# Attention tiles of a fused layer: one set of four transposes moved behind the first block of a projection, another set moved ahead of a projection

## What is computed

```
q, k, v = x @ Wq, x @ Wk, x @ Wv            # 16 heads of 32
q, k = rotate(silu(q)), rotate(silu(k))
# in chunks of 128 rows, with a running state S per head
scores = (q_i @ k_i.T) * D
o_i    = scores @ v_i + (q_i * decay_q) @ S
S      = lam_C * S + (k_i * decay_k).T @ v_i
o = group_rmsnorm(o * sigmoid(x @ Wg1 @ Wg2)) * weight
x = x + o @ Wo
# feed-forward: 512 -> 4096 (gate and up, 4-bit weights) -> 512
x = x + (gelu(gate) * up) @ Wdown
```

## Time and profile before

| | |
|---|---|
| median of three runs | 1288.63 us |
| profiled execution | 1288.75 us, of which the span from first to last instruction 1286.7 us |
| TensorE busy | 1270.3 us (99%) |
| VectorE busy | 917.0 us (71%) |
| ScalarE busy | 475.2 us (37%) |
| GpSimd busy | 435.2 us (34%) |
| granted TensorE clock | 1.00 over the span |
| attention part | about 9 to 310 us |

### The profile page before, as it was taken

The page is one execution under the profiler, slowest core; times in us unless marked ns, Lnnn a source line. Parts: engine busy times, 40 slices in busy tenths (PEclk is TensorE's granted clock), DMA queues, the critical chain, the costliest instruction groups (busy, mean ns, idle before and its releaser), DMA issues.

```text
span 1286.7 us, 20699 instructions
## 1 busy us (share of the span) xinstructions
PE 1270.3 (99%) x7376; PEld 1043.5 (81%) x7376; DVE 917.0 (71%) x1594; ACT 475.2 (37%) x799; POOL 435.2 (34%) x360
## 2 busy tenths in 40 slices
PE   9999999998999999999999999999999999999998
PEld 6888888887788888888888888888888888888887
DVE  7878788788867667676767676767767666767665
ACT  5433434434433333333333433333333333333421
POOL 2434455564442322223132324133232324232400
PEclk9999999999999999999999999999999999999999
DMA  9000000000001000010000000001001000000003
GB/s 326 12 2 1 19 17 2 2 1 2 25 25 33 17 33 27 22 33 28 29 24 24 24 24 24 33 16 33 24 24 33 24 33 24 24 24 24 24 13 119
DMA packets 21778, 40.23 MB, mean 31 GB/s; under 512 B 2660, under 2 KB 2916, under 8 KB 21604
## 3 DMA queue, kind: packets, MB, share of 16 engines
q1 hardware_dynamic: 21060, 39.47, 9.4%
q10 hardware_dynamic: 672, 0.13, 0.1%
HBM read 35.40 MB, written 4.19 MB: 31 GB/s over the span
## 4 chain that ended last, share of the span: by engine, by line
PE 93%; DVE 2%; POOL 1%; ACT 1%; issue 1%; POOLq 0%; DVEq 0%; ACTq 0%
PE bank L1351 16%; PE bank L1354 15%; PE bank L1353 15%; PE bank L1197 13%; PE bank L1199 13%; PE bank L1198 13%; PE bank L1211 2%; PE bank L1291 1%; PE bank L1310 1%; PE bank L1300 1%; PE bank L1343 1%; PE bank L1331 1%; PE bank L1258 0%; ACT xg L394 0%; PE bank L1257 0%
## 5 line engine op out<-in xcount | busy, mean ns | idle before, releaser
L883 DVE TENSOR_TENSOR acc<-acc,bank 128x512 f32<-128x512 f32 x248 | 169.3, 683 | 129.4 <-PE bank L1199 129.3
L1197 PE MATMUL bank<-wdh,hh 128*128 128x512 f32 x512 | 199.3, 389 | 0.0
L1199 PE MATMUL bank<-wdh,hl 128*128 128x512 f32 x512 | 199.2, 389 | 0.0
L1198 PE MATMUL bank<-wdl,hh 128*128 128x512 f32 x512 | 199.2, 389 | 0.0
L1351 PE MATMUL bank<-xoh,wgh 128*128 128x512 f32 x448 | 175.9, 393 | 0.6 <-DVE cxa L891 0.6
L1351 PE MATMUL bank<-xoh,wuh 128*128 128x512 f32 x448 | 175.1, 391 | 0.7 <-ACT cxa L482 0.7
L1354 PE MATMUL bank<-xoh,wgl 128*128 128x512 f32 x448 | 174.5, 390 | 0.0
L1354 PE MATMUL bank<-xoh,wul 128*128 128x512 f32 x448 | 174.3, 389 | 0.0
L1353 PE MATMUL bank<-xol,wuh 128*128 128x512 f32 x448 | 174.3, 389 | 0.0
L1353 PE MATMUL bank<-xol,wgh 128*128 128x512 f32 x448 | 174.3, 389 | 0.0
L899 DVE TENSOR_TENSOR hl<-hx,hh 128x512 fp32r<-128x512 f32 x128 | 113.5, 887 | 51.4 <-ACT hh L489 51.0
(11 more groups left out here) (163 smaller groups left out, 2285.7 us busy)
## 6 DMA issues: line engine op xcount, KB each, us to landing
stg<-packed_dram SPq DMA_DIRECT2D x48, 256.0 KB, 2.5
stg<-scales_dram SPq DMA_DIRECT2D x48, 256.0 KB
out_dram<-acc SPq DMA_DIRECT2D x16, 256.0 KB, 2.0
acc<-x_dram SPq DMA_DIRECT2D x3, 1024.0 KB, 15.0
w_in<-wq_dram SPq DMA_DIRECT2D x2, 512.0 KB, 5.2
w_in<-wk_dram SPq DMA_DIRECT2D x2, 512.0 KB, 6.9
w_in<-wv_dram SPq DMA_DIRECT2D x2, 512.0 KB, 8.6
w_in<-wo_dram SPq DMA_DIRECT2D x2, 512.0 KB, 11.2
```

The lines of the kernel that those rows point to most:

```text
L883: V.tensor_tensor(row, row, BY[j % 2][:], ALU.add).then_inc(y_add, 1)
L1197: pe.matmul(dst, w_h, x_h, start=start, stop=False)
L1198: pe.matmul(dst, w_h, x_l, start=False, stop=False)
L1199: return pe.matmul(dst, w_l, x_h, start=False, stop=stop)
```

## The change

`o_back(t)` of a tile with c below 3 moves from ahead of the q projection of tile t+2 to behind its first block of three matmuls. (Tile 0 has an order of its own, which stays; where c is 3 it stays behind the second block.) `o_transpose(t-1)` moves from behind the v projection of tile t+1 to ahead of it, in tiles 1 to 13; `passage` already has it there for tile 14. On ScalarE the copy `ot_hi_(t-1)` moves ahead of `v_copy(t+1)`, and on VectorE `gate_low(t+1)` moves behind `rope_of`, both from tile 1 on. No instruction is added or removed.

```
 ScalarE, tile(b, c)
                 if at_start(b, c):
                     xt_hi_(2)
+                else:
+                    ot_hi_(t - 1)
                 v_copy(t + 1, (c + 1) % 2)
                 if not at_start(b, c):
-                    ot_hi_(t - 1)
                     xt_hi_(t + 2)
 VectorE, tile(b, c)
                 decayed_q(t)
-                gate_low(t + 1)
                 if at_start(b, c):
+                    gate_low(t + 1)
                     xt_lo_(2)
                 rope_of(b, c, t + 1, (c + 1) % CHUNKS)
+                if not at_start(b, c):
+                    gate_low(t + 1)
                 if not at_start(b, c):
                     ot_lo_(t - 1)
 TensorE, tile(b, c)
                 else:
+                    o_transpose(t - 1)
                     pe.wait_ge(st_done, kvs(b, c))
                 v_project(t + 1)
-                if not at_start(b, c):
-                    o_transpose(t - 1)
...
-                if c < CHUNKS - 1:
-                    o_back(t)
                 q_ready(t + 2)
                 for k in range(KT):
-                    if c == CHUNKS - 1 and k == 2:
+                    if k == (1 if c < CHUNKS - 1 else 2):
                         o_back(t)
                     q_part(k)
```

## The result

The changed kernel takes 1294.78 us (median of 6 runs, 1292.77 to 1295.47), the kernel before 1288.72 on the same chip (6 runs, 1288.38 to 1292.15). The ratio is 1.0039, with a 95% interval of 1.0026 to 1.0051: slower by 0.39%. The profiled execution took 1295.47 us with a span of 1293.4, against 1288.75 and 1286.7; that is 6.7 us more, and the following reading accounts for these 6.7.

What follows compares the result with a forecast made beforehand. TensorE's queue was taken as the bound (busy 1270.3 us, VectorE 917.0). New waits of 8.4 us less gains of 5.2 gave +3.1 us, 1291.8 us against the median of 1288.63; range 1288.2 to 1293.4.

Steps and rivals of the forecast that it cites:

- `o_back`'s wait: At `o_back` in ten tiles, the 0.42 us wait for ScalarE's copy vanishes; net about 0.39 us saved a tile.
- Gains: On TensorE: 3.9 us from `o_back`, 0.85 from `o_transpose`, 0.47 ahead of tile 8's output projection and scores; 5.2 us.
- The new waits: `o_transpose` ahead of the v projection waits for the multiply writing `sq` in tiles 1, 5, 8, 10, 13, 14; 8.4 us.
- The double hold in tile 10: GpSimd's rotation holds VectorE's last small Newton step, then its second half holds the multiply; TensorE waits 3.88 us.
- The row of tile 12: Trace example of a held VectorE small step: 0.66 us instead of 0.17 beside GpSimd's sum.
- `gate_low` behind `rope_of`: On VectorE, `gate_low` ends 1.6 to 2.8 us after the silu, scores start 2.8 after it; no time added.
- The sum: Whole kernel: waits 8.4 us less gains 5.2, net +3.1 us, giving 1291.8; feed-forward part only starts later.
- One hold or none: Fewer GpSimd holds in tiles 8 and 10: +1.7 us with one each, -0.3 with none; chance 0.37.
- The multiply in time: VectorE's chain comes forward with TensorE, so all six waits vanish; about 1283.8 us, chance 0.11.
- `o_back` still waiting: Dearer q projection restart takes up to 3.9 us from the gains, ending at 1295.7; small chance within the 0.52 for slower.

Runs made afterwards that it cites:

- the stands filled: Changed kernel plus 9 and 15 extra unread matmuls just before `o_transpose` in tiles 8 and 10, keeping TensorE busy; 1291.39 us, ratio 1.0022.
- the repeat: The changed kernel measured once more with no edit; 1292.88 us, ratio 1.0036 against the kernel before.
- the fastest kernel: Changed kernel with `o_transpose` late in tiles 1, 5, 8, 10, 13 and the passage, and GpSimd's rotation waiting for the multiply in tile 10; 1284.46 us.

## Why the prediction was right in direction and wrong in size

- **`o_back`'s wait.** Right. It is gone in all ten tiles; 0.42 us a tile instead of the 0.39 forecast.
- **Gains.** 5.87 us came out against 5.2. `o_back` gave 0.3 more. The x transposes now take 0.41 us up to the output projection in every tile, instead of 0.47 to 0.53 outside tile 8, which is some 0.8 us; the forecast gave them a gain in tile 8 alone, and why they are shorter elsewhere isn't shown. Against this, an early `o_transpose` that needn't wait saved 0.05 to 0.07 us and not 0.09, and the output projection became about 0.03 longer in most tiles. Read stage by stage the gains add up to 6.0.
- **The new waits.** Right, tile by tile: forecast 0.90, 0.63, 2.42, 3.88, 0.16 and 0.39, measured 0.89, 0.69, 2.40, 3.64, 0.43 and 0.38. The method, TensorE's arrival at the new place subtracted from the multiply's end, was off by 0.27 at most. That largest miss, tile 13, has a reason: `gated` of tile 12 follows `o_back` itself (VectorE is idle for 1.22 us there, waiting for it, instead of 0.97), and the forecast allowed for that in the tiles without a wait but not in tile 13.
- **The double hold in tile 10.** Right, and its cause was where the forecast put it: the experiment with `o_back` alone has it, the one without `o_back`'s move hasn't, and a GpSimd that waits takes it away. The rule that the forecast weighed, the Trainium skill's page SBUF — State Buffer, section "SBUF: two separate sides", by which the small step is held as well, agrees with the 1.13 us of the trace. The row of tile 12 that the forecast leaned on the earlier trace rows is one of GpSimd's subtractions for the feed-forward part (L1141) and not its sum of the rotation (L1059), as the forecast has it; as an example of a held small step it serves as well.
- **`gate_low` behind `rope_of`.** Right for the changed kernel, where its place makes no difference that can be told. "Nothing is added" holds only while `o_transpose` waits first: with `o_transpose` late, 1.5 to 1.6 us of waiting for `g` appeared.
- **The sum: the step that failed.** "Waits [...] 8.4; gains 5.2; net +3.1 us", with the feed-forward part "otherwise the same", took each matmul behind a wait at the duration that it has today. Two v projections behind the long stands took 1.58 us more each, at the lower clock: 3.2 us in the profiled execution, which no case and no bound of the range contained. With the stands filled, the kernel was 2.2 us over before by the medians and 3.0 between the profiled spans, against the +3.1 forecast. The rows read beforehand had no stand of this length in tiles 1 to 13, and the stands of the passage (1.17 and 1.02 us) had a clock of 1.00 around them. The forecast gave this cost nothing; it should have bounded it: at half clock a v projection costs up to its own length again. In the four executions with a mean clock of 0.999 the kernel ends near 1292.8, inside the range; in most of the first measurement's it was 0.996 or 0.997. That the repeat's median lies inside the range is luck and no support for the sum, which had no low stretch in it.
- **The rivals.** One hold or none: tile 10 had both, so no. The multiply in time: no, the waits came to 8.4 us, not under 2.6. `o_back` still waiting: no.

Two things stay open. Why the clock stayed full behind a wait of 2.23 us in one profiled kernel and fell behind the same wait in three others isn't settled by these runs. Nor is it settled why it is sometimes lower in the passage. Twelve of the thirteen profiled executions, the kernel before among them, have stands of 1.14 to 1.17 and 1.02 us there, with eight transposes between them. The clock stayed full in nine of these and fell in three: GpSimd waiting in tiles 8 and 10, `o_transpose` late in tiles 8 and 10 with `gate_low` behind, and the fastest kernel. So no length of a stand can be named from these runs below which the clock is safe.

## What to carry to other kernels

When an instruction moves ahead on the bound engine, subtract its arrival at the new place from the end of what it needs, tile by tile: here it gave six waits within 0.3 us, and showed that the move pays in eight tiles and not in the others. A long wait on TensorE can have a second price in the matmuls behind it, here 1.58 us behind waits of 2.2 us and more in all but one case; so count it once as waiting, and put the lower clock into the range. A shift of 0.4 us can turn the order in which GpSimd and VectorE meet; look at both engines around each multiply that the bound engine waits for, and if needed let GpSimd wait for it.

## What the runs showed of the hardware that was not expected

- TensorE's granted clock fell to its lower level behind stands of 2.2 and 3.5 us within otherwise dense work. Eight matmuls were then 0.43 us apart instead of 0.23, and 1.58 us were lost each time. Behind single stands of 1.09, 1.24, 1.49 and 1.63 us it stayed full. It fell behind 2.23 us in three profiled executions and not in a fourth, and behind 3.47 to 3.67 us in all three. The Trainium skill, page TensorE: Matmul & The Clock Gate, section "Part 1: The HAM clock gate (the "warmup" mystery)", says that an idle TensorE is throttled to half rate and that work releases the throttle; the traces agree, with 0.43 us a matmul behind the stands and 0.23 to 0.24 again from 177.31 us on in tile 8 of the repeat. Of the change to the full rate the section says that its point varies from run to run; what varied here is whether the clock fell at all.
- Stands in two pieces did the same. Behind 0.68 and 1.50 us, with four transposes between them, the scores took 2.09 us instead of 1.17. Behind 1.16 and 1.02 us, with eight transposes between them, the clock fell in three profiled executions of twelve, and 1.2 us were lost in the one shown.
- A VectorE step over 128x16 elements took 1.13 to 1.31 us beside GpSimd's rotation instead of 0.17, and got its turn between the two halves of GpSimd's work: the small step ended at 211.59 in the changed kernel, and the multiply queued behind it was held by the second half.
- Between two executions of the same kernel VectorE's small steps in the passage were held differently (four of 0.52 to 0.65 us from 333.65 us on in one, none over 0.29 in the other), and TensorE waited 1.53 us there in the first and 0.24 in the second.
